# Attention with 16 heads and a routed expert layer in one launch: another way to finish the attended values

## The reference, cut to what matters

```python
xn  = layernorm(x)                                   # x: 2 x 1024 x 512, float32
out = x + attention(xn) + ffn(xn)

def attention(x, Wq, Wk, Wv, Wo):                    # 16 heads of 32 features
    S = einsum('bhqd,bhkd->bhqk', Q, K) / sqrt(32); S = where(causal, S, -1e30)
    P = softmax(S)
    return (P @ V).transpose(0, 2, 1, 3).reshape(b, t, 512) @ Wo.T

def ffn(x):      # 8 experts of width 352, the two best of each token, and a shared one of width 704
    return sum_e cw[:, e] * (silu(x @ gate_e.T) * (x @ up_e.T)) @ down_e.T + shared(x)
```

## Time and profile before

| | us |
|---|---|
| median of 3 runs (lowest, highest) | 1117.6 (1117.13, 1122.85) |
| profiled execution, its own time | 1127.01 |
| its span | 1125.0 |
| PE busy in the span | 1046.2 (93%) |
| DVE, ACT, POOL busy | 784.6, 637.9, 506.4 |
| attend, from its first matmul to its last value matmul | 183 to 758 |
| out, to its last matmul | 761 to 819 |

### The profile page before, as it was taken

The page is one execution under the profiler, slowest core; times in us unless marked ns, Lnnn a source line. Parts: engine busy times, 40 slices in busy tenths (PEclk is TensorE's granted clock), DMA queues, the critical chain, the costliest instruction groups (busy, mean ns, idle before and its releaser), DMA issues. The chain is left out here.

```text
span 1125.0 us, 18890 instructions
## 1 busy us (share of the span) xinstructions
PE 1046.2 (93%) x5379; PEld 817.6 (73%) x5380; DVE 784.6 (70%) x1675; ACT 637.9 (57%) x1278; POOL 506.4 (45%) x568
## 2 busy tenths in 40 slices
PE   6999979888899998999999999998989999999994
PEld 4767867666677776777778777776867777778872
DVE  6732324565688887788888888865568888888872
ACT  3323211265588786787787887872155555565550
POOL 0013903388756564556566565651013443333321
PEclk9999989988899999999999999998989999999997
DMA  6989996255543553644445426118789444443432
GB/s 213 322 335 361 136 293 231 94 67 102 132 133 77 150 148 75 163 118 136 115 113 151 126 64 191 45 39 266 243 283 278 90 76 75 75 72 68 71 54 35
DMA packets 106201, 163.61 MB, mean 145 GB/s; under 512 B 53984, under 2 KB 64480, under 8 KB 102656
## 3 DMA queue, kind: packets, MB, share of 16 engines
q1 hardware_dynamic: 95776, 141.82, 44.1%
q0 software_dynamic: 9760, 20.49, 10.0%
q10 hardware_dynamic: 576, 0.26, 0.1%
HBM read 101.25 MB, written 61.28 MB: 144 GB/s over the span
## 5 line engine op out<-in xcount | busy, mean ns | idle before, releaser
L1198 POOL TENSOR_TENSOR prob_lo<-prob,prob_hi 128x512 fp32r<-128x512 f32 (+2 forms) x320 | 308.3, 977 | 203.3 <-ACT prob_hi L1243 147.0
L1236 ACT ACTIVATE prob<-ps_s 128x512 f32<-128x512 f32 (+3 forms) x384 | 188.0, 490 | 127.1 <-PE ps_s L1463 77.1
L1243 ACT ACTIVATE prob_hi<-prob 128x512 fp32r<-128x512 f32 (+3 forms) x384 | 198.6, 517 | 12.4 <-ACT row_stage L1217 12.4
L1862 DVE TENSOR_TENSOR rw_lo<-gu_sb,rw_hi 128x704 fp32r<-128x704 f32 x156 | 138.8, 893 | 52.7 <-ACT rw_hi L1806 47.7
L1306 DVE CUSTOM_DVE_ANT_0 ps_m<-ps_m,causal 128x384 f32<-128x384 f32 (+3 forms) x256 | 126.7, 495 | 69.2 <-PE ps_m L1432 66.9
L1806 ACT ACTIVATE rw_hi<-gu_sb 128x704 fp32r x156 | 123.5, 794 | 62.8 <-PE ps_ru L1895 43.6
L1458 PE MATMUL ps_s<-qs,ks 97*128 97x512 f32 (+3 forms) x384 | 140.4, 366 | 9.4 <-ACT prob L1236 9.2
L1779 POOL DMA_INDIRECT out<-work,slot_table x39 | 63.5, 1627 | 181.1 <-DVE work L1847 148.2
L1481 PE MATMUL ps_o<-prob_hi,vs 128*66 128x512 f32 (+3 forms) x384 | 133.1, 347 | 10.4 <-issue 9.6
L1432 PE MATMUL ps_m<-ks,qs 96*128 96x512 f32 (+3 forms) x384 | 139.1, 362 | 0.6 <-DVE maxima L1306 0.2
L1483 PE MATMUL ps_o<-prob_lo,vs 128*66 128x512 f32 (+3 forms) x384 | 132.0, 344 | 0.0
(11 more groups left out here) (201 smaller groups left out, 2353.0 us busy)
## 6 DMA issues: line engine op xcount, KB each, us to landing
xt<-xt_blocks SPq DMA_DIRECT2D x7, 2048.0 KB, 9.1
v_rows<-work SPq DMA_DIRECT2D x16, 512.0 KB, 3.0
xt_blocks<-xt SPq DMA_DIRECT2D x4, 2048.0 KB, 11.3
qk_hi<-work SPq DMA_DIRECT2D x8, 1024.0 KB, 4.7
qk_lo<-work SPq DMA_DIRECT2D x8, 1024.0 KB, 7.5
qs<-qk_hi SPq DMA_DIRECT2D x64, 128.0 KB, 2.9
ks<-qk_hi SPq DMA_DIRECT2D x64, 128.0 KB, 3.2
vs<-v_rows SPq DMA_DIRECT2D x32, 256.0 KB, 4.7
```

The lines of the kernel that those rows point to most:

```text
L1198: nc.gpsimd.tensor_tensor(prob_lo[:, s % NPL, 0:w], prob[:, s % NP, 0:w], prob_hi[:, s % NPH, 0:w].bitcast(F32), ALU.subtract).then_inc(lo ...
L1236: nc.scalar.activation(prob[:, s % NP, 0:w], ps_s[s % NS][:, 0:w], ACT.Exp, scale=SCALE).then_inc(exp_done, 1)
L1243: nc.scalar.activation(prob_hi[:, s % NPH, 0:w], prob[:, s % NP, 0:w], ACT.Copy).then_inc(hi_ready, 1)
L1862: nc.vector.tensor_tensor(w_lo[:, k, :], chunk(e, k), w_hi[:, k, :].bitcast(F32), ALU.subtract).then_inc(w_lo_ready, 1)
```

## The change

- `attended` is laid out by feature: partition = feature within a chunk of four heads ("quad"), free = tile, chunk, query. The order of heads is four heads of a quad for batch 0, the same four for batch 1, then the next quad (`head_of`).
- At the end of a half, `o_copy` is not transposed. Two steps after the value matmul SP moves its 32 high rows into `attended` and its 32 low rows into a tile `low` by DMA, at the partitions of that head, and its row of sums to DRAM (`place_output`, three DMAs, 64 times).
- When the four heads of a quad are there, 16 times in all: SP loads the quad's 4 x 512 sums as 128 x 16 (`load_sums`), DVE inverts them (`invert`), SP stores them to DRAM (`save_inverses`) and loads each head's 512 back to 32 partitions (`spread_inverses`, four DMAs), DVE adds `low` (`sum_outputs`, 128 x 512) and multiplies (`normalize`, 128 x 512). The last of the 16 is done in out, at tiles 0 to 6, and the last four tiles wait for it.
- SP's program in attend goes by steps instead of by heads; `load_xt`, `store_acc`, `load_base` and `load_gate_up` stand at the step at which what they wait for is due. `vs` has two slots instead of four.
- Wo is loaded in attend when the shared expert's last up matmul is done, and split there by ACT and DVE, into the place of the shared expert's gate and up weights.
- Out has no copy, no transposes and no splitting of Wo: ACT and DVE take the high and low part straight from `attended`. Its loops are written out.
- The planner's 270 ns for the output transposes are gone, and with them the steps at which the shared expert's matmuls stand move a little.

```diff
+def head_of(g):
+    return QUAD * (g // (QUAD * B)) + g % QUAD, g // QUAD % B
 ...
+    def load_sums(self, sp, k):
+        sp.wait_ge(self.sums_saved[k % 2], 16 * QUAD * (k // 2 + 1))
+        sp.dma_start(self.halves[k % 2].sums[:, :], self.sums_dram[k:k + 1, :]...)
+    def invert(self, dve, k):
+        dve.wait_ge(self.sums_loaded[k % 2], 16 * (k // 2 + 1))
+        self.nc.vector.reciprocal(sums[:, :], sums[:, :]).then_inc(self.inverted, 1)
+    def save_inverses(self, sp, k):
+        sp.wait_ge(self.inverted, k + 1)
+        sp.dma_start(self.inv_dram[k:k + 1, :]..., self.halves[k % 2].sums[:, :])
+    def spread_inverses(self, sp, k):
+        sp.wait_ge(self.inv_saved[k % 2], 16 * (k // 2 + 1))
+        for n in range(QUAD):
+            sp.dma_start(self.halves[k % 2].inverse[n * DK:(n + 1) * DK]..., ....broadcast_to([DK, TBW]))
+    def sum_outputs(self, dve, k):
+        dve.wait_ge(self.o_placed[k % 2], 32 * QUAD * (k // 2 + 1))
+        self.nc.vector.tensor_tensor(of, of, self.halves[k % 2].low[:, :, :], ALU.add)
+    def normalize(self, dve, k):
+        dve.wait_ge(self.inv_spread[k % 2], 16 * QUAD * (k // 2 + 1))
+        self.nc.vector.tensor_tensor(of, of, self.halves[k % 2].inverse[:, :, :], ALU.mult)
 ...
-    COPY, TURN, NORM = VALUE + 1, VALUE + 2, VALUE + 3
+    COPY, PLACE = VALUE + 1, VALUE + 2
+    SUMS, INVERT, SAVE, SPREAD, SUM, NORM = [VALUE + n for n in (4, 6, 7, 9, 10, 11)]
 ...
-        if 0 <= s - TURN < STEPS and (s - TURN) % NB in ENDS:
-            cost += 270
 ...
+    WO_AT = step_of(UNITS - 1, UP_END[-1] - 1) + 2
+    WO_SPLIT_AT = {WO_AT + 8 + 2 * k: k for k in range(KC)}
+    XT_AT = {step_of(unit - 1, UP_END[-1] - 1) + 1: unit for unit in range(1, UNITS)}
+    STORE_AT = {step_of(unit, PER_UNIT - 1) + 2: unit for unit in range(UNITS)}
+    BASE_AT = {0: 0, **{s + 4: unit + 1 for s, unit in STORE_AT.items() if unit + 1 < UNITS}}
+    RAW_AT = {NB: 0, **{s + 2: ks[0] + 1 for s, ks in SPLIT_AT.items() if ks[0] + 1 < NF}}
 ...
+                for s in range(ALL):                       # sync engine, attend
+                    if s % NB == 0 and HS <= s // NB + 1 < HEADS:
+                        next_head(s // NB + 1)
+                    if s % NB == NB // 2 and V_SLOTS <= s // NB - 1 < HEADS:
+                        load_values(s // NB - 1)
+                    if 0 <= s - PLACE < STEPS:
+                        place_output(s - PLACE)
+                    for lag, stage in ((SUMS, finish.load_sums), (SAVE, finish.save_inverses),
+                                       (SPREAD, finish.spread_inverses)):
+                        if finished(s - lag):
+                            stage(sp, quad_half(s - lag))
+                    ...                                    # load_wo, load_xt, store_acc, load_base, ...
 ...
-                pipeline(dve, NT, U, [(0, copy), (1, lo), (1, split_wo), (2, add)])
+                pipeline(dve, NT, U, [(0, lo), (0, last_outputs), (1, add)], back=NT)
-                pipeline(pe, NT, U, [(0, turn), (1, multiply)])
+                pipeline(pe, NT, U, [(0, multiply)], back=NT)
```

More of the change, by code:

```diff
@@ L20 @@
 from concourse import mybir
+from collections import namedtuple
 from contextlib import ExitStack
@@ L97, in moe_attention_kernel @@
     slots_dram = nc.dram_tensor("slots", [NSLOT, 2], F32, kind="Internal").ap()
+    sums_dram, inv_dram = [nc.dram_tensor(name, [2 * B * H // QUAD, QUAD * TBW], F32, kind="Internal").ap()
+                           for name in ("sums", "inverses")]
     xt_dram = nc.dram_tensor("xt_blocks", [NTB, P, 2, KC, TBW], F32, kind="Internal").ap()
@@ L986, in load_values, with place_output @@
                 def load_values(g):
-                    c, h, b = g % HS, g // B, g % B
-                    wait(sp, pv_done, NB * (g - HS + 1))
+                    c, (h, b) = g % V_SLOTS, head_of(g)
+                    wait(sp, pv_done, NB * (g - V_SLOTS + 1))
                     sp.dma_start(vs[:, c, :, 0:2 * DK].bitcast(F32),
                                  v_dram[:, b * QT:(b + 1) * QT, h, :]).then_inc(values_loaded[c], 16)
+                def place_output(s):
+                    if s % NB not in ENDS:
+                        return
+                    g, half = s // NB, BLOCKS[s % NB][0]
+                    (h, b), n = head_of(g), g % QUAD
+                    at = slice(n * DK, (n + 1) * DK)
+                    if g == 0 and half == 0:
+                        for stored in qk_stored:
+                            sp.wait_ge(stored, 32 * (2 * D // P // len(qk_stored)))
+                    sp.wait_ge(o_copied, 2 * g + half + 1)
+                    if n == 0:
+                        wait(sp, finish.o_ready, 2 * (g // QUAD - 1) + half + 1)
+                    tiles = slice(b * QT + 4 * half, b * QT + 4 * half + 4)
+                    for into, rows in ((attended[at, tiles, h // QUAD, :], slice(0, DK)),
+                                       (halves[half].low[at], slice(DK, 2 * DK))):
+                        sp.dma_start(into, o_copy[rows, half, :].rearrange("p (a q) -> p a q", a=4)
+                                     ).then_inc(finish.o_placed[half], 16)
+                    k = 2 * (g // QUAD) + half
+                    sp.dma_start(sums_dram[k:k + 1, n * TBW:(n + 1) * TBW],
+                                 o_copy[2 * DK:2 * DK + 1, half, :]).then_inc(finish.sums_saved[half], 16)
                 def load_xt(unit):
@@ L1033, in _ @@
                                      ).then_inc(table_loaded, 16)
[L1034 to L1040, removed]
-                    if 0 < g <= HEADS:
-                        load_values(g - 1)
-                    for k in range(NF):
-                        if g == RAW_AT[k]:
-                            load_gate_up(k)
-                        if g == DOWN_RAW_AT[k]:
-                            load_shared_down(k)
-                store_acc(UNITS - 1)
                 sp.wait_ge(acc_stored, 64 * UNITS)
@@ L1484, in value @@
                                      stop=n in ENDS).then_inc(pv_done, 1)
-                def turn_o(s):
-                    if s % NB not in ENDS:
-                        return
-                    o = 2 * (s // NB) + BLOCKS[s % NB][0]
-                    pe.wait_ge(o_copied, o + 1)
-                    wait(pe, o_read, o)
-                    wait(pe, row_ready, turned["rows"])
-                    for q in range(4):
-                        last = nc.tensor.transpose(ps_ot[:, q, 0:VW], o_copy[:, o % 2, q * P:(q + 1) * P],
-                                                   ident[0:VW, 0:VW])
-                    last.then_inc(o_turned, 1)
-                    turned["outputs"] += 1
                 def gate_or_up(unit, m):
@@ L1600, in _ @@
             def _(sp):
-                for k in range(KC):
-                    sp.dma_start(wo_raw[:, k, :], wo[:, k, :]).then_inc(wo_loaded[k], 16)
                 def load(i, c):
```

290 lines of the change are left out of this document (162 added, 128 removed).

## The result

The changed kernel takes 1137.73 us (median of 4 runs, 1132.83 to 1143.76) against 1118.64 (4 runs, 1117.13 to 1122.85): the ratio is 1.016, with a 95% interval of 1.012 to 1.020. I had forecast 1103.7. It is slower.

What follows compares the result with a forecast made beforehand. PE was taken as the bound, except from 234 to 300 us (POOL). The terms -12.4 - 8 + 8 - 1.5 = -13.9 us took 1117.6 to 1103.7; forecast range 1096 to 1111, 8 in 10 range 1089 to 1115.

Steps and rivals of the forecast that it cites:

- the new waits on DVE: Attend: DVE's reciprocal and product wait for DMAs; PE feels 6.6 us, plus 1.4 for a lower clock: +8 us.
- R1: Rival: waits at the reciprocal and product of all 15 halves cost 62 us, kernel about 1158; chance 0.08.
- the pass-through: In attend, PE, waiting for maxima with two PSUM banks, feels about D - 1.7 of a DVE wait of D us.
- The estimate of +3: Attend: with about 2 us a DMA, every chain is 0.5 to 1 us shorter and the DVE-wait term nearer +3.
- Behind large blocks: Attend: chain transfers queued behind large ones make DVE wait 2.5, 2.8, 5.6 and 2.5 us; PE feels 6.6.
- Transposes, -12.4: Output transposes removed: 57 groups from 300 to 755 us, where PE sets the pace, save 12.4 us.
- Step-wise SP, -8: Attend: PE gaps at 426, 447.6 and 469.8 us from late raw weights and xt go: -8, ends -4 and -9.
- DVE work, worth 0: Attend: 110 us of DVE work gone, 29 new; worth 0 by itself, but shortens the catching-up after a wait.
- End of attend, +7: An unhidden DMA chain for the half before the last ends attend 7 us later, between 4 and 11.
- out, -1.5 in sum: Output projection with end of attend: +2.1 later start, -5.6 transposes, +2 y tile wait; -1.5, between -6 and +4.
- R2: Rival: ACT takes over the pace, half of the transposes' gain stays, 1110; chance 0.10.
- R4: Rival: new gaps where PE wants `y_acc` or `o_copy` too soon; half the 8 lost, 1108; chance 0.58 with the forecast.

Runs made afterwards that it cites:

- e2_nochain: The changed kernel without the DMA chain of the inverses for the 15 halves finished in attend, all DVE operations kept: 1099.39 us, ratio 0.980 to the kernel before.
- e5_savefirst: The changed kernel with SP's sums load, inverse save and spread ahead of the next head's loads in each step: 1129.96 us, ratio 1.010 to the kernel before.
- e9_normlag: The changed kernel with only the product five steps later (lag 16 instead of 11): 1135.37 us, ratio 1.014 to the kernel before.
- e10_place: The changed kernel with only SP's placement of the next quad waiting for the last quad's sum, not its product: 1131.29 us, ratio 1.010 to the kernel before.
- e6_latesum: The changed kernel with the product five steps later and SP's placement waiting for the sum, not the product: 1103.24 us, ratio 0.986 to the kernel before.
- e3_spsteps: The kernel before with nothing but SP's attend program by steps: 1115.62 us, ratio 0.995 to the kernel before.
- e1_late: The changed kernel with sum and product three steps later (lags 13 and 14 instead of 10 and 11): 1131.28 us, ratio 1.009 to the kernel before.

## Why the prediction was wrong

**The step that failed: "the new waits on DVE", term +8.** By e2_nochain the chain costs +36.9 in 26 heads, 29 more than I had put: 23.8 us of idle PE where I had 6.6, and 13.1 us of slower matmuls where I had 1.4. With +37 in its place my own sum gives +15 for the kernel, and +19 was measured between the medians. R1, "DVE's waits decide", was the case, and I gave it 0.08. Four errors are in the term.

First, the pass-through. I let PE feel D - 1.7 of a wait of D. At head 22 D is 2.89 and PE stands 3.42. Over the seven waits for the inverses in the heads, D adds up to 23.1 us and PE stands for 19.7 behind them; my rule gives 11.6 for these waits. The likely reason is read from the timeline and not tested by itself: the 1.7 us of lead was free time on DVE, and the change fills the same stretch with its own work, sum 1.45 and product 1.31, both longer than the 0.79 I took. Lag 10 and 11 put them on both sides of one maximum.

Second, the chain. I had the arrival of DVE right (6.1 us from the reciprocal to the product's turn; 6.5 forecast), but the spreads' landing at 8.96 us after the reciprocal where the sum had 7 to 8.2. The usual landing is not to blame: by the table of DMA issues (count, KB, median us to landing) it is at most my 2.8.

```profile
work<-o_copy SPq DMA_DIRECT2D x63, 64.0 KB, 2.1
...
o_inv<-inverses SPq DMA_DIRECT2D x56, 64.0 KB, 2.1
...
sums<-sums SPq DMA_DIRECT2D x14, 8.0 KB, 2.8
inverses<-sums SPq DMA_DIRECT2D x14, 8.0 KB, 1.8
```

It is what stands ahead of a transfer in its place: the save behind a head's six loads was issued at 584.46 and SP was free to spread at 588.57, 4.1 us; the spreads behind an xt block took 5.4. And SP itself stands in line, for the placement and for DVE's reciprocal (L64 and L253 above, 48.8 us in all, of which a part delays nothing). The first chain, to the reciprocal, where I had "no wait", was late too: DVE waits 2.92 us for the sums in head 9 and 3.21 in head 25. With the save ahead of the loads (e5_savefirst) SP's wait for the saved inverses falls from 18.2 us to the 11.5 below, but DVE's 27.5 stay:

```profile
SPq L64 <- DVE work L273: 21.6, 6, 7.8
...
SPq L259 <- DMA inverses<-sums: 11.5, 9, 1.9
```

I had made one landing for all, "decides from about 3.9", the condition of R1; the median was 2.1 and R1's mechanism came true all the same. The constant of about 2 us that the Trainium skill gives (DMA: Bandwidth & Descriptors, "Anatomy of one DMA") is fitted there to transfers that GpSimd issues; the rows of SP's small transfers, 1.8 to 2.8 us, agree with it. The estimate of +3 that I drew from it was further off than my own.

Third, the loop. I walked each half's chain alone. L1108 makes SP wait for DVE's last product and L273 makes DVE wait for SP's spread; e9_normlag and e10_place show that loosening either end alone leaves the kernel at 1.014 and 1.010, and e6_latesum, with both, is at 0.986. I named what is queued behind DVE's waits, but not what is queued on SP behind a wait for DVE.

Fourth, the clock. A stop costs more than it lasts: beyond its idle time a disturbed head is 0.4 us longer (head 6) to 3.3 us (head 26: 20.88 us, 2.82 of it idle, against 14.81 in e6_latesum), and matmuls take 0.63 for 0.39 after it. I had put 1.4 once for all, and it is 13.1.

**Behind large blocks**: expected at the xt and `store_acc` places, and seen. The longest wait, 5.74 us at 527.11, is that of spreads issued at 519.94 behind an xt block of 517.75; I had 5.6 for the third such place. The last spread was issued by 521.7 and landed at 527.1, 5.4 us where 2.1 is the median. That agrees with the rule of the Trainium skill on rings that the prediction names, as far as these rows go.

**Transposes, -12.4**: right, a little small. Undisturbed heads went from 15.4 to 14.85, which over 28 heads is -15. (The 15.8 that I named as the distance of before was that of one pair of head loads, and so 15.3 was too high.)

**Step-wise SP, -8**: right within its range; e3_spsteps has -7.3 in the heads and -5.3 in time. The waits of ACT for raw weights are gone, but heads 11 to 13, in each of which a part of the shared weights is split, still take 17.4 to 18.1 with 2.5 to 2.6 us idle each.

**DVE work, worth 0**: no run tests it by itself. By instruction durations the outputs took 112 us before and take 38 now (110 and 29 forecast), and DVE is busy 56 us less; that "they shorten the catching-up" did not help where the new operations stood in a cluster.

**End of attend, +7, and out, -1.5 in sum**: the sum is near, from the last value matmul to the first routed one -0.2, but by luck, since two errors cancel. The first matmul of the projection comes only 0.4 us later behind the last value matmul than before (7.6 us for 7.2), where I had 4.4; and from it to the projection's last matmul PE gains only 0.6 us (53.2 for 53.9), where I had 5.9. The last product waits 4.41 us (770.37). The third y tile stalls PE for 3.89 at 790.11 where I had +2 at the fifth, and two slow tiles follow:

```profile
770.37 0.69 DVE L273 TENSOR_TENSOR work<-work,o_inv 128x512 f32<-128x512 f32 x1 [4.41 <-DMA o_inv<-inverses]
...
788.77 0.69 DVE L1776 TENSOR_TENSOR y_tile<-ps_ay,y_tile 128x512 f32<-128x512 f32 x1 [6.59 <-DMA y_tile<-out]
```
The 7.6 us are not the 11 that I named as a sign either; without the chain it is 4.7 (e2_nochain), so the chain costs 2.9 there. Undisturbed tiles are 2.72 apart (2.78 forecast).

**ACT as the pace (R2)**: not seen. In e2_nochain ACT has 81.92 of 100 us and PE 98.77. **Gaps that move (R4)**: seen, but small. Heads 11 to 13 take 51.9 us in e2_nochain, 6.7 of them idle, and 49.6 in e3_spsteps, with 2.2 idle.

**What stays open.** Heads 0 to 5 became 3.4 us shorter; e3_spsteps leaves them (107.6) and e2_nochain keeps the gain (104.7), so it is not of SP's order or the chain. All of it lies in head 0 (20.7 us before, 17.3 after), which ends at 222.7 in the trace of before, ahead of the first transposes of an output at 234.1. So it is neither the transposes nor DVE's relief; the planner's other places for the shared expert's matmuls are left, which no run tries alone. Why e5's order keeps the waits at 27.5 us I did not follow through all halves. e6_latesum still has 405.0 where e2_nochain has 398.2; heads 9, 13, 18 and 25 hold 5.9 of these 6.8 us, idle 2.8 more in all over the 26 heads, and the rest is slower matmuls.

## What to carry to other kernels

An engine's slack can be used once: before a wait of D us is priced at "D less the lead", take the new instructions around it off the lead as well. Where engine A waits for a transfer of B and B's queue waits for A, draw the cycle over one period with what stands between in both queues, and loosen both ends in one experiment: here each alone left the kernel slower than before. Ask of such a wait which operation really is the last reader. And price a stop of TensorE with what follows it; over a third of what the chain cost in the heads was matmuls at a lower clock. The cheapest test of a new chain is to leave it out and keep its arithmetic: e2_nochain gave cost and gain of the change in one experiment.

## What was not expected of the hardware

The same 128 x 512 operation on DVE (the sum or the product) took 0.68 to 0.69 us where GpSimd had nothing to do or began later, and 0.75 to 1.79 us where a GpSimd operation was well under way at its start. By lines, 184 to 780 us (busy, mean ns, idle before):

```profile
L266 DVE TENSOR_TENSOR work<-work,o_low 128x512 f32<-128x512 f32 x15 | 18.5, 1234 | 0.0
L273 DVE TENSOR_TENSOR work<-work,o_inv 128x512 f32<-128x512 f32 x15 | 14.1, 938 | 27.5 <-DMA o_inv<-inverses 27.5
```

Two starts show who waits for whom. In the changed kernel a GpSimd operation is under way from 586.85, the sum starts at 586.96 and takes 1.45 us, ending 0.55 us after the GpSimd operation; at 765.28, with GpSimd done, it takes 0.68. In e1_late, last line, the sum starts first, at 327.24, and takes 0.69 us; the GpSimd operation behind it takes 1.72, where the same form takes 1.26 to 1.30 undisturbed:

```profile
586.85 1.01 POOL L1335 TENSOR_TENSOR prob_lo<-prob,prob_hi 128x384 fp32r<-128x384 f32 x1
...
327.36 1.72 POOL L1335 TENSOR_TENSOR prob_lo<-prob,prob_hi 128x512 fp32r<-128x512 f32 x1 [0.68 <-ACT prob_hi L1380]
```

The Trainium skill (SBUF — State Buffer, "SBUF: two separate sides") says that a DVE operation with two inputs in SBUF and a GpSimd operation that reads SBUF lock each other out for a whole instruction; the rows agree with it, in both orders. My 0.79 was the mean of another line, the low part of `prob`, and stood for operations that start beside GpSimd.

The start of attend moves between executions: head 0 began at 195.8 to 203.0 us in 14 traces whose programs differ little before that point. One profile against one profile can mislead by that much, so stretches between marks are compared here.
